# Expert results weighted as they leave PSUM and added into the output by a scattering DMA

## The reference

```python
p = jax.nn.sigmoid(x @ gate_w.T)
p = p / jnp.sum(p, axis=-1, keepdims=True)
w, idx = jax.lax.top_k(p, 2)
w = w / jnp.sum(w, axis=-1, keepdims=True)
combine = jnp.sum(jax.nn.one_hot(idx, 16) * w[..., None], axis=1)
gate, up = jnp.split(jnp.einsum('th,ehf->etf', x, gate_up_proj), 2, axis=-1)
y = jnp.einsum('eti,eih->eth', silu(gate) * up, down_proj)
out = residual + jnp.einsum('eth,te->th', y, combine)
```

## Time and profile before

| what | value |
|---|---|
| median of 3 runs | 2274.36 us |
| profiled execution | 2273.29 us, span 2271.6 us |
| TensorE busy | 2137.9 us, 94% of the span |
| DVE busy | 1554.3 us, 68% |
| ACT busy | 1260.9 us, 56% |
| POOL busy | 560.4 us, 25% |
| last stage, from its barrier | 1945.85 to 2271.6 us |
| DMA queue of SP (q1) | 173.60 MB, 21.9% of the engines' span |
| DMA queue of POOL (q0) | 16.80 MB, 2.2% |

### The profile page before, as it was taken

One profiled execution on the slowest core, in us unless ns is written; L12 is line 12 of the kernel. 1 busy time (PEld: TensorE's weight loads), 2 busy tenths in 40 slices (PEclk: granted clock), 3 DMA queues, 4 the chain that ended last, 5 costly groups with the idle time before them and its releaser, 6 DMA issues. The chain is left out here.

```text
span 2271.6 us, 38211 instructions
## 1 busy us (share of the span) xinstructions
PE 2137.9 (94%) x12318; PEld 1864.9 (82%) x12318; DVE 1554.3 (68%) x3798; ACT 1260.9 (56%) x3373; POOL 560.4 (25%) x1274
## 2 busy tenths in 40 slices
PE   5999999999999899998999999999999999589993
PEld 4899999999999678887788888888888888378882
DVE  6777777777778884434666666666666667867776
ACT  4555455455454533323666666666666666567772
POOL 1000001001000122223333333333333333144541
PEclk8999999999999999999999999999999999789997
DMA  6122111111210220002111111111111110278886
GB/s 254 65 80 80 46 69 63 61 69 46 78 57 27 70 75 1 1 1 75 47 56 47 56 63 57 46 55 46 55 46 55 58 55 36 83 246 293 291 277 259
DMA packets 74388, 195.83 MB, mean 86 GB/s; under 512 B 8448, under 2 KB 39192, under 8 KB 61488
## 3 DMA queue, kind: packets, MB, share of 16 engines
q1 hardware_dynamic: 64432, 173.60, 21.9%
q0 software_dynamic: 7680, 16.80, 2.2%
q10 hardware_dynamic: 2176, 4.19, 0.5%
HBM read 177.78 MB, written 25.17 MB: 89 GB/s over the span
## 5 line engine op out<-in xcount | busy, mean ns | idle before, releaser
L608 PE MATMUL bank<-l_wkv_hi,l_ctxT 128*128 128x256 f32 (+1 forms) x1024 | 278.8, 344 | 7.0 <-DMA l_ctxT<-ctx_split 5.2
L1025 DVE TENSOR_TENSOR l_v_lo<-bank,l_v_hi 128x128 fp32r<-128x128 f32 (+1 forms) x256 | 91.7, 358 | 213.5 <-ACT l_v_hi L847 212.2
L1025 DVE TENSOR_TENSOR l_pT_lo<-bank,l_pT_hi 128x512 fp32r<-128x512 f32 x256 | 175.2, 684 | 77.9 <-ACT l_pT_hi L872 77.9
L866 ACT ACTIVATE l_probs<-l_scored,l_nbias 128x256 f32<-128x256 f32 x256 | 128.2, 502 | 158.6 <-DVE l_nbias L1078 155.6
L608 PE MATMUL bank<-l_wo_hi,l_oT_hi 128*128 128x512 f32 x512 | 209.3, 409 | 0.7 <-DVE l_oT_lo L1025 0.7
L608 PE MATMUL bank<-xnT_hi,l_wq_hi 128*128 128x512 f32 x512 | 209.8, 410 | 0.0
L608 PEld LDWEIGHTS bank<-l_wkv_hi,l_ctxT 128*128 128x128 f32 x1024 | 183.3, 193 | 28.2 <-issue 6.3
L608 PE MATMUL bank<-xnT_lo,l_wq_hi 128*128 128x512 f32 x512 | 201.7, 394 | 0.0
L608 PE MATMUL bank<-xnT_hi,l_wq_lo 128*128 128x512 f32 x512 | 201.7, 394 | 0.0
L608 PE MATMUL bank<-l_wo_hi,l_oT_lo 128*128 128x512 f32 x512 | 201.1, 393 | 0.0
L608 PE MATMUL bank<-l_wo_lo,l_oT_hi 128*128 128x512 f32 x512 | 200.8, 392 | 0.0
(11 more groups left out here) (288 smaller groups left out, 5949.9 us busy)
## 6 DMA issues: line engine op xcount, KB each, us to landing
l_ctxT<-ctx_split SPq DMA_DIRECT2D x64, 1024.0 KB, 4.8
moe_raw_gu<-in_L_ffn_gate_up_proj SPq DMA_DIRECT2D x32, 1024.0 KB
moe_raw_dn<-in_L_ffn_down_proj SPq DMA_DIRECT2D x32, 512.0 KB
l_raw_a<-in_L_xattn_Wq SPq DMA_DIRECT2D x16, 512.0 KB, 5.8
l_raw_a<-in_L_xattn_Wo SPq DMA_DIRECT2D x16, 512.0 KB, 5.4
x_sb<-in_x SPq DMA_DIRECT2D x4, 1024.0 KB, 11.1
ctx_split<-ct SPq DMA_DIRECT2D x4, 1024.0 KB, 13.6
moe_raw_gu<-moe_y_rows SPq DMA_DIRECT2D x4, 1024.0 KB
```

The lines of the kernel that those rows point to most:

```text
L608: mm = nc.tensor.matmul(out, a[x], b[y], start=(i == 0), stop=(i == n - 1))
L866: ins = nc.scalar.activation(probs[u % 2][:, t, :], src, ACT.Exp, bias=nbias[:, i:i + 1], scale=scale, accum_out=rsum[:, i:i + 1])
L1025: nc.vector.tensor_tensor(pair[1], src, pair[0].bitcast(F32), ALU.subtract).then_inc(done, 1)
```

## The change

`y_rows`, the loads back and the additions after the loop are gone, and so are the stores behind them. Instead SP stores the residual to the output at the start of the stage. The routing weights of each token are written behind its normed row in DRAM (`xn_rows` has 514 columns), so that a gather brings them along, and DVE picks of the two the one that the slot stands for (`weigh`). `copy_y` multiplies by it on the way out of PSUM. POOL scatters with an addition into the output, at the token's row. A token has two choices, in different experts, so two adds may meet in one row and must not be in flight together. Halves 3j and 3j+1 hold rows of one expert, so no token twice: their adds aren't ordered among themselves. The add of 3j+2 waits until both have landed, and the next two wait until that one has. Result buffers are six, and POOL issues the adds eight halves behind the gather.

```diff
+    LAG = 8
+    out_rows = out.rearrange("b s d -> (b s) d")
...
+        y_sb += [at_place(f"y_sb{STEPS + i}", y_at + 4 * D * i, [P, D], F32) for i in range(STEPS)]
...
+            for n in range(NT // 2):
+                sp.dma_start(out_v[:, 2 * n:2 * (n + 1), :], k.x_sb[:, 2 * n:2 * (n + 1), :]).then_inc(stored, 16)
             for t in range(LATE, NT):
                 wait_normed(sp, t)
-                sp.dma_start(rows_v[:, t, :], xn[:, t, :]).then_inc(rows_out[t // TG % 2], 16)
-            sp.wait_ge(experts_set, 1)
+                sp.dma_start(rows_v[:, t, 0:D], xn[:, t, :]).then_inc(rows_out[t // TG % 2], 16)
+            sp.wait_ge(rows_found, 2)
+            sp.dma_start(rows_v[:, :, D:D + 2], weights[:, :, :]).then_inc(rows_out[1], 16)
+            sp.wait_ge(listed, 1)
...
-            for n in range(NT // 2):
-                due(sp, summed, 2 * (n - 5))
-                sp.dma_start(both_rows[n % 6].rearrange("p (t c) -> p t c", t=2), yv[:, 2 * n:2 * (n + 1), :]).then_inc(both_in[n % 6], 16)
+            sp.wait_ge(stored, 16 * NT // 2)
...
             def gather_rows(n):
-                due(pool, x_turned, n - 2)
+                due(pool, weights_set, n - 2)
...
-            def scatter(n):
+            def add_rows(n):
+                j, part = n // STEPS, n % STEPS
                 pool.wait_ge(y_copied, n + 1)
+                if n == 0:
+                    pool.wait_ge(stored, 16 * NT // 2)
+                elif part == 0:
+                    pool.wait_ge(y_out[2], 16 * j)
+                elif part == 2:
+                    pool.wait_ge(y_out[0], 16 * (j + 1))
+                    pool.wait_ge(y_out[1], 16 * (j + 1))
                 apart(k, pool)
-                at = bass.IndirectOffsetOnAxis(ap=dest_of[:, column_of(n)], axis=0)
-                gp.indirect_dma_start(y_rows, at, y_sb[n % STEPS][:, :], None, bounds_check=2 * T - 1, oob_is_err=False).then_inc(y_out[n % STEPS], 16)
-
-            for r in rows_out:
-                pool.wait_ge(r, 16 * TG)
-            pool.wait_ge(listed, 2)
-            for n in range(HALVES + 2 * STEPS):
+                at = bass.IndirectOffsetOnAxis(ap=token_of[:, column_of(n)], axis=0)
+                gp.indirect_dma_start(out_rows, at, y_sb[n % (2 * STEPS)][:, :], None, bounds_check=T - 1, oob_is_err=False,
+                                      compute_op=ALU.add).then_inc(y_out[part], 16)
+
+            for r, loads in zip(rows_out, (TG, TG + 1)):
+                pool.wait_ge(r, 16 * loads)
+            pool.wait_ge(listed, 3)
+            for n in range(HALVES + LAG - 1):
                 if n < HALVES:
                     gather_rows(n)
-                if n >= 2 * STEPS:
-                    scatter(n - 2 * STEPS)
+                part = (n - LAG) % STEPS
+                if n >= LAG and part == 0:
+                    add_rows(n - LAG)
+                    add_rows(n - LAG + 1)
+                elif n >= LAG and part == 1:
+                    add_rows(n - LAG + 1)
...
             def copy_y(n):
                 act.wait_ge(y_made, n + 1)
-                due(act, y_out[n % STEPS], 16 * (n // STEPS))
-                nc.scalar.copy(y_sb[n % STEPS][:, :], b_y[n % 2][:, :]).then_inc(y_copied, 1)
+                due(act, y_out[n % STEPS], 16 * (n // STEPS - 1))
+                act.wait_ge(weights_set, n + 1)
+                nc.scalar.activation(y_sb[n % (2 * STEPS)][:, :], b_y[n % 2][:, :], ACT.Identity, scale=weight_of[:, n:n + 1]).then_inc(y_copied, 1)
...
-            for i in range(len(PARTS)):
-                find_quotients(i)
-                find_rows(i)
+            find_quotients(0)
+            find_rows(0)
+            chain(v.tensor_tensor(ms[:, :], m1[:, :], m2[:, :], ALU.add))
+            chain(v.reciprocal(ms[:, :], ms[:, :]))
+            chain(v.tensor_tensor(weights[:, :, 0], m1[:, :], ms[:, :], ALU.mult))
+            v.tensor_tensor(weights[:, :, 1], m2[:, :], ms[:, :], ALU.mult).then_inc(rows_found, 1)
+            find_quotients(1)
+            find_rows(1)
...
+            chain(v.tensor_scalar(choice_bit[:, :], dest_of[:, :].bitcast(U32), 1, None, ALU.bitwise_and))
+            chain(v.tensor_copy(choice[:, :], choice_bit[:, :]))
+            chain(v.tensor_scalar(other[:, :], choice[:, :], -1.0, 1.0, ALU.mult, ALU.add))
+
+            def weigh(n):
+                pair, at = rows[n % STEPS][:, D:D + 2], slice(n, n + 1)
+                c = column_of(n)
+                chain(v.tensor_tensor(second_part[:, at], pair[:, 1:2], choice[:, c], ALU.mult))
+                v.scalar_tensor_tensor(weight_of[:, at], pair[:, 0:1], other[:, c], second_part[:, at], ALU.mult, ALU.add).then_inc(weights_set, 1)
...
                                 xT[n % 2][0].bitcast(F32), ALU.subtract).then_inc(x_split, 1)
+                weigh(n)
...
-            for t in range(NT):
-                n = t // 2
-                if t % 2 == 0:
-                    dve.wait_ge(both_in[n % 6], 16 * (loads_before[n % 6] + n // 6 + 1))
-                for c, weight in enumerate((m1, m2)):
...
-        xn_rows = nc.dram_tensor("xn_rows", (T, D), F32, kind="Internal").ap()
+        xn_rows = nc.dram_tensor("xn_rows", (T, D + 2), F32, kind="Internal").ap()
```

More of the change, by code:

```diff
@@ L1765, in moe_stage @@
     ACT_TILES = [t for t in range(LATE, NT) if t not in DVE_TILES]
-    y_rows = nc.dram_tensor("moe_y_rows", (2 * T, D), F32, kind="Internal").ap()
+    out_rows = out.rearrange("b s d -> (b s) d")
+    out_v = out.rearrange("b (t p) d -> p (b t) d", p=P)
     gu_v = gate_up.rearrange("e (p k) f -> e p (k f)", p=P)
@@ L1790, in moe_stage @@
         by_half = [at_place(f"by_half{c}", dn_at + 4 * DN * (2 + c), [P, NT, 2, HALVES], BF16) for c in range(2)]
-        rows = [sb(f"rows{i}", [P, D]) for i in range(STEPS)]
+        rows = [sb(f"rows{i}", [P, D + 2]) for i in range(STEPS)]
         xT = [[x[:, :, P * i:P * (i + 1)] for x in (k.xnT_hi, k.xnT_lo)] for i in range(2)]
@@ L1797, in moe_stage @@
         y_sb = [sb(f"y_sb{i}", [P, D]) for i in range(STEPS)]
+        weights = sb("weights", [P, NT, 2])
+        choice_bit, choice, other = sb("choice_bit", [P, HALVES], U32), sb("choice", [P, HALVES]), sb("other", [P, HALVES])
+        second_part, weight_of = sb("second_part", [P, HALVES]), sb("weight_of", [P, HALVES])
         token_of, dest_of, expert_of = sb("token_of", [P, HALVES], I32), sb("dest_of", [P, HALVES], I32), sb("expert_of", [P, 2 * PAIRS], I32)
@@ L1851, in due @@
                 eng.wait_ge(s, n)
-        both_rows = [raw_gu[0][:, :], raw_gu[1][:, :]] + [w[i][:, :].bitcast(F32) for w in w_gu for i in range(2)]
         is_half = rows[0][:, 0:NT * HALVES // 2].bitcast(BF16).rearrange("p (t j) -> p t j", j=HALVES)
@@ L2028, in turn_x @@
                 due(pe, x_split, n - 1)
-                by_feature = rows[n % STEPS][:, :].rearrange("p (q k) -> p k q", k=KD)
+                by_feature = rows[n % STEPS][:, 0:D].rearrange("p (q k) -> p k q", k=KD)
                 for c in range(KD):
@@ L2203, in _ @@
             copy_y(HALVES - 1)
-            ov = out.rearrange("b (t p) d -> p (b t) d", p=P)
-            for n in range(NT // 2):
-                act.wait_ge(summed, 2 * (n + 1))
-                act.dma_start(ov[:, 2 * n:2 * (n + 1), :], k.x_sb[:, 2 * n:2 * (n + 1), :]).then_inc(stored, 16)
-            act.wait_ge(stored, 16 * NT // 2)
         @block.vector
```

44 lines of the change are left out of this document (16 added, 28 removed).

## The result

| | before | changed |
|---|---|---|
| time, median (lowest to highest), us | 2274.36 (2271.98 to 2275.61) | 2285.46 (2278.53 to 2287.98) |
| profiled execution, us | 2273.29 | 2286.21 |
| its span, us | 2271.6 | 2284.5 |

The ratio is 1.0047, 95% interval 1.0029 to 1.0065: slower by half a per cent, where 1.4% faster was forecast. The changed kernel's stretches answer to the earlier trace rows (window, length, us of each engine and instructions, clock, DMA share, GB/s); the row from 2010 to 2220 lies inside the loop.

What follows compares the result with a forecast made beforehand. Loop bound by TensorE at 4.85 us a half, the end by reading 8 MB back, adding and storing 4 MB. -32.0 + 0.1 + 0.36 = -31.5 gave 2242.9, with slips 2243 us; range 2239.5 to 2260, its own 2240 to 2247.

Steps and rivals of the forecast that it cites:

- The tail: After the loop: loads back, additions and stores go, last add lands at 2239.45 instead of an end at 2271.6: -32.0 us.
- 0.1 for the end of the program: After the last add lands: 0.1 us until the program ends, taken off a gain of 32.15 us.
- the upper bound: Last adds: extra landing time of an add over a plain scatter, bounds 0 and 2.1 us, 0.6 taken.
- POOL, in the loop: Ordered adds on POOL's queue: chain of 13.7 us fits a three-half round of 14.56 us by 0.9; cost 0.
- 3.1 + 2L: POOL's loop: 1.3 us between a pair's adds, two landings, 0.9 us after each; 13.7 us a round.
- L: Landing time of an add in the loop: 4.7 us from one loaded scatter, with 0.6 for adding: 5.3 us.
- the 0.6 for adding: Each add's landing: 0.6 us more than a plain scatter, about one more pass over the bytes.
- Rival A: In the loop: ordering chain mildly becomes the bound, 1.3 us over the round, +15 us, time 2258; chance 0.15.
- About 6 us of slip in all are free: POOL's loop: early gathers and six result buffers absorb about 6 us of total delay at no cost.
- Rival B: In the loop: ordered landings take 8 us each, +35 us, time 2310; decides from L = 6.9; chance 0.08.
- DMA engines, in the loop: Share 0.85 rises to 0.95 or 1.06 with extra passes; adds delay themselves rather than the weights; cost 0.
- ACT, DVE, SP: Scaled copy +0.1 us at the end; DVE weight operations +0.36 before the loop, 0 in it; SP's startup stores 0.

Runs made afterwards that it cites:

- few loads: Changed kernel without the weight loads of experts 2 to 15, order and adds kept: 2251.05 us, ratio 0.9903.
- without order: Changed kernel with halves sent to their own internal rows, waiting only for the same part one expert earlier: adds 2245.20 us, plain stores 2246.59 us.
- two orderings: Changed kernel with plain stores into internal rows in place of adds, its ordering waits kept: 2248.19 us, ratio 0.9885.
- one ordering: Changed kernel with adds into internal rows, the third waiting for its pair but the next pair not for the third: 2272.11 us, ratio 0.9994.
- adds one by one: Changed kernel with unordered adds into internal rows, one after each gather instead of two back to back: 2246.14 us, ratio 0.9884.
- with six buffers: Changed kernel with only the third waiting for its pair, adds into internal rows, six gather buffers instead of three: 2266.16 us, ratio 0.9963.

## Why the prediction was wrong

**The tail, -32.0 forecast.** The loads, additions and stores went as it says. What came in their place was mis-sized. The kernel with few loads shows the tail by itself, since its loop is undisturbed: TensorE ends at 2233.1, the span at 2248.0, 15.0 us against 6.4.

```profile
2233.05 1.56 POOL L1965 DMA_INDIRECT out_x<-moe_y_sb,moe_token_of  x1 [2.02 <-ACT moe_y_sb L2192]
...
2241.09 1.56 POOL L1965 DMA_INDIRECT out_x<-moe_y_sb,moe_token_of  x1 [4.62 <-DMA out_x<-moe_y_sb,moe_token_of]
```

Three errors. The pair had to wait for the landing of add 44, an empty third, at 2232.21 (the row names ACT, whose copy of half 46 ended at the same moment; that of half 45, which the add needs, had ended 2.4 us before it). So add 46 starts at 2234.91, not 2233.21: +1.7; without order it starts at 2233.39. It lands in 5.25 us, not 2.7: +2.55. And "0.1 for the end of the program" took 4.2: +4.1. In between the third add starts 0.93 us after that landing and lands in 2.74 us, both as forecast. Together 8.5. In the changed kernel the last pair, moreover, starts 4.5 us after TensorE's end, since the chain lags behind. The second of the last pair as a plain store (two orderings), then as an add (few loads), both on quiet engines:

```profile
2233.81 2.73 DMA moe_y_rows<-moe_y_sb,moe_dest_of
```

```profile
2234.91 5.25 DMA out_x<-moe_y_sb,moe_token_of
```

2.5 us more, above the 2.1 that I gave as the upper bound. I had taken the landing from the earlier trace rows, that of half 47, a third without a row. For such a one 0.65 more is what is measured (2.74 against 2.09 us), but it can't be the adding of data: POOL's instruction alone takes 0.54 us longer (1.56 against 1.02).

**POOL, in the loop, cost 0 forecast.** This is the step that failed, +32 us: "The chain in it: 3.1 + 2L", with L = 5.3, 13.7 us. Measured, means of 13 rounds: 2.07 from add to add, 6.85 for the second to land, 0.96 until the third starts, 6.29 for it to land, 1.19 until the next pair: 17.36. The term that was mis-sized is L: 6.6 on average, 1.3 too short and in the sum twice, 2.5 of the 3.7 us. The second add of a pair came 2.07 behind the first, not 1.3: another 0.8. The 0.9 from a landing to the next start was right (0.96, and 1.19 to the next pair): 0.35.

L was short for two reasons. The 4.7 us came from one scatter of the kernel before; the mean of its first 39 is 5.35, and that was on record. And the 0.6 for adding had nothing in it for two DMAs back to back: without order, plain stores in pairs take 6.7 on average and adds in pairs 7.8. With 0.9 us of room, a long landing (one in ten takes over 8.6 us) isn't given back either.

I also looked for one loop only. That POOL's queue, with the work of its own instructions, is a second loop of 15.8 us (one ordering) wasn't in the prediction. Rival A's mechanism was the right one, at less than half its true size: 2.8 us a round, not 1.3.

**"About 6 us of slip in all are free"** was near: 36.4 us of slip cost 31.8.

**Rival B** (slower, 2310) was right in sign and place, wrong in its mechanism: an add doesn't take 8 us by itself (5.25 on quiet engines). Its point of decision, L = 6.9, holds only if L is worked back from the round, which puts the late second add into it: (17.36 - 3.1) / 2 = 7.1. The landings themselves take 6.6.

**DMA engines, in the loop, cost 0.** Right, though the reason was poor: shares of 0.92 (adds in pairs) and 0.96 (adds one by one) without order cost nothing.

**ACT, DVE, SP.** Cost as forecast, with small misses. DVE's weight operations stand at 1972.28 to 1973.2, the first gather is 0.84 us late (0.36 forecast), the residual's stores were issued from 1947.21 on and the rows were written by 1966.5 (1963.5 forecast). The store of the weights' 2048 pieces was mis-sized, to the safe side: issued at 1973.19, done by 1975.6, at 7 ns of one engine's time a packet, where the forecast's 3.2 ns for all 16 are 51 of one. The row is the hardware queue's from 1974.2 to 1975.6 (packets, MB, share).

```profile
q1 hardware_dynamic: 2001, 0.02, 64.4%
```

The Trainium skill's rule on transfers below 512 bytes ("DMA: Bandwidth & Descriptors", section Specifications), cited in the prediction, would have given more; the store took 2.4 us from issue to end, and shows no sign of it.

## What to carry to other kernels

An order between DMAs is paid for on the queue of the engine that issues them. Before you add one, write down that engine's round as a loop: every instruction in it, every wait with a landing time measured for that very kind of transfer, full and under the loop's own traffic, and the reaction after it; if the room that is left is less than what your landing times may be wrong by (here 0.9 us of room, and twice 1.3 us of error), don't put the cost at nothing; order against something a whole round old instead, if need be into a second destination. An ordered DMA that moves no row is waited for like any other. Look for the second loop of about the same length before you take the first away.

## What I had not expected of the hardware

- An accumulating DMA moves a row of 2048 bytes in 178 ns on an engine (median; mean 215 in the changed kernel's loop), where plain rows go two in a 4096-byte packet of 159: 2.2 times per byte. POOL's issue of 128 such rows takes 1.56 us against 1.02.
- After the last software DMA the program doesn't end at once: in the changed kernel the last add lands at 2280.3 and the span ends at 2284.5, and in every other run that ends with an indirect add it is 4.2 us too. With plain scatters it is 7.0 us after the landing (2236.7 to 2243.7). In the kernel before the same piece lay under the loads back, where the page doesn't show it.
- From the last data packet of a landing to the start of the add that waited for it no less than 1.2 us pass: some 0.35 to the last semaphore update, then 0.88 to 0.94.
- An indirect DMA without a row to move takes 2.7 us to land on quiet engines and up to 8.6 beside the loads of the changed kernel.
- Left open: why a single ordering makes the time vary so much between runs (2253 to 2277 with six buffers), and how the landings of a round depend on where the loads fall in it.
